# Pair attention on one core: the outputs of a past pair ahead of scores and transposed scores in each half slot

## The chip, the cores and the metric

The kernel runs on one NeuronCore of a Trainium2 chip. Its engines work side by side, each in the order of its own instruction stream, and wait for each other on semaphores: PE is TensorE (matmuls; PEld is its weight loads), DVE is VectorE, ACT is ScalarE, POOL is GpSimd, SP issues DMAs. The metric is the device time of one execution in microseconds (us); lower is better.

## The reference

The program is four layers of cross attention and feed-forward over `x` (8 batches, 256 tokens, width 128) with a context of 8 x 512 tokens. Two of the eight phases have the shape that the change touches, 16 heads of width 8, with 256 queries and 512 keys in each of the 8 batches. Cut to these:

```python
def _L1_xattn_ref(values, keys, query, mask, Wv, Wk, Wq, Wo, bo):
    v = (values @ Wv.T).reshape(n, -1, H, D)
    k = (keys @ Wk.T).reshape(n, -1, H, D)
    q = (query @ Wq.T).reshape(n, lq, H, D)
    score = jnp.einsum('nqhd,nkhd->nhqk', q, k)
    score = jnp.where(mask == 0, jnp.float32(-1e+20), score)
    attn = jax.nn.softmax(score / jnp.sqrt(jnp.float32(D)), axis=-1)
    out = jnp.einsum('nhqk,nkhd->nqhd', attn, v).reshape(n, lq, H * D)
    return out @ Wo.T + bo

def _L3_xattn_ref(query, key, value, temporal_bias, wq, bq, wk, bk, wv, bv, wo, bo):
    logits = jnp.einsum('bhqd,bhkd->bhqk', q, k) / scale
    logits = logits + temporal_bias[:, None, None, :]
    attn = jax.nn.softmax(logits, axis=-1)
    ...
x = x + _L1_xattn_ref(ctx_1024, ctx_1024, _layernorm(x, axis=-1), mask, ...)
...
x = x + _L3_xattn_ref(_layernorm(x, axis=-1), ctx_1024, ctx_1024, fside_BxS2_0, ...)
```

## The kernel before

Nine phases run one after the other. `pair_attention` (line 758) builds two of them: tag `l1x`, with a mask (`masked`), and tag `l3x`, with a bias of the keys in place of a mask (`biased`). I call them the masked and the biased attention.

Its unit is a pair of heads. There are 8 pairs in a batch and 8 batches, so T = 64 pairs, numbered t. All engines walk the same slots t = -7 .. 69, each cut into two half slots j = 0, 1. I number half slots h = 2t + j. A pair passes through these steps:

- `scores(t + LEAD, j, (w,))`, seven slots early: one matmul for each head w of the pair, from 128 queries against 512 keys, into bank `s_ps[w]`. Their only use is the row maximum, which DVE takes (`maximum`, lines 1069 and 1072) and which frees the bank.
- After four pairs, POOL splits their maxima into three bf16 parts (`mparts`, lines 643 to 649), PE turns them (job MX, line 1220), ACT copies them, and two DMAs put them as extra rows under the queries.
- `transposed_scores(t, j, (1 - w,))`: the scores again, with keys on the partitions and the maximum already taken off, into `st_ps[j]` (line 1255). In the masked attention `mask_scores(t, j)` first puts the mask into that bank (line 1242) and the transposed scores are added to it.
- ACT: `exponential(t, j)` reads `st_ps[j]` and writes `pT` (line 1131). It does so one half slot later in its own order.
- `outputs(group, c)`: a group is two pairs, that is four heads. For each of four chunks c of 128 keys, four heads' outputs and softmax sums are accumulated into the single bank `pv_ps` (line 1282). Chunks 0 to 3 of group g stand in half slots 4g + 4 to 4g + 7, so each half slot has one chunk.
- ACT: `copy_outputs(g)` (line 1139) takes the finished group out of `pv_ps`.
- `fill(job, b, n)`: small jobs through the one bank `misc`, at most one in a half slot: XT and Q make the queries of a batch, K and V its keys and values, MX turns maxima, OT, ONT and OUT finish a batch.

Two waits and one place in ACT's order matter. Chunk 0 of a group overwrites `pv_ps`, so it waits for the copy of the group before:

```python
pe.wait_ge(*m.exp_done.after(2 * (2 * group + 1) + c // 2 + 1))
if c == 0:
    if group:
        pe.wait_ge(*m.pv_copied.after(group))
```

And ACT's loop has that copy behind the exponential of the half slot before:

```python
before = t - 1 + j
if 0 <= before < T:
    exponential(before, 1 - j)
if j == 0 and t >= 4 and t % 2 == 0 and (t - 4) // 2 < T // 2:
    copy_outputs((t - 4) // 2)
job, b, half = filled_at.get(2 * t + j - 1, (None, 0, 0))
```

So at h = 8, 12, 16, .., 128 (31 of them) ACT does `exponential` of half slot h - 1, then the copy of the group that ended at h - 1, then the drain of the job of h - 1. The jobs of a batch b stand at 16b - 35 (K), 16b - 34 (XT), 16b - 32 (Q), 16b - 1 (V), 16b - 5 and 16b + 2 (MX), 16b + 20 and 16b + 22 (OT), 16b + 24 (ONT), 16b + 25 (OUT).

Of the kernel before, what the change touches and what calls it, by code (L numbers as in the profile page):

```python
# [757 lines left out]
def pair_attention(m, tag, wq, wk, wv, wo, bo, bq=None, bk=None, bv=None, mask=None, mask_t=None, key_bias=None, follow=None):  # L758
# [3 lines left out]
    T = B * PP  # L762
# [29 lines left out]
    with ExitStack() as ctx:  # L792
# [62 lines left out]
        with nc.Block() as block:  # L855
            @block.sync
            def _(sp):
# [13 lines left out]
                def stack_k(b, w):  # L871
                    if w == 0:
                        sp.wait_ge(*m.k_split.after(b - 1))
                        if b >= NST:
                            sp.wait_ge(*m.st_filled.after(2 * PP * (b - NST + 1)))
                    for row, _, of_k in STACK:
                        sp.dma_start(kT[b % NST][64 * w + row:64 * w + row + HD, :, :], parts[64 * w:64 * w + 64, of_k, 0:KV])\
                            .then_inc(m.stack_landed[b % NST].sem, 16)
                    if biased:
                        sp.dma_start(kT[b % NST][64 * w + 48:64 * w + 51, :, :],  # L880
                                     kb_rows[3 * b:3 * b + 3, :].unsqueeze(1).to_broadcast([3, PP, KV]))\
                            .then_inc(m.stack_landed[b % NST].sem, 16)
# [74 lines left out]
            def _(pool):  # L957
# [79 lines left out]
                for _, step, args in sorted(order, key=lambda s: s[0]):  # L1037
                    step(*args)
# [156 lines left out]
            def _(pe):  # L1195
# [39 lines left out]
                def mask_scores(t, j):  # L1235
                    b, p = divmod(t, PP)
                    if t >= 1:
                        pe.wait_ge(*m.exp_done.after(2 * t + j - 1))
                    if p == 0 and j == 0:
                        pe.wait_ge(*m.mask_t_ready.after(b + 1))  # L1240
                    for w in range(2):
                        pe.matmul(st_ps[j][:, w, :], k["ident_bf"], maskT_b[b % 2][:, 2 * j:2 * j + 2, :].rearrange("p c t -> p (c t)"),  # L1242
                                  start=True, stop=False)

                def transposed_scores(t, j, heads=(0, 1)):
                    b, p = divmod(t, PP)
                    if t >= 1 and heads[0] == FIRST_TURNED and not masked:
                        pe.wait_ge(*m.exp_done.after(2 * t + j - 1))
                    if j == 0 and p % 4 == 0 and heads[0] == FIRST_TURNED:
                        pe.wait_ge(*landed(m.max_moved, 2 * b + p // 4, 32))  # L1250
                    for e in range(2):
                        c = 2 * j + e
                        for w in heads:
                            rows = slice(64 * w, 64 * w + R2)
                            ins = pe.matmul(st_ps[j][:, w, e * S:(e + 1) * S], kT[b % NST][rows, p, c * P:(c + 1) * P], q[b % NST][rows, p, :],  # L1255
                                            start=not masked, stop=not masked or e == 1)
                    if len(heads) == 2 or heads[0] != FIRST_TURNED:
                        ins.then_inc(m.st_filled.sem, 1)

                def scores(t, j, heads=(0, 1)):  # L1260
                    b, p = divmod(t, PP)
                    if p == 0 and j == 0 and heads[0] == 0:
                        pe.wait_ge(*stack_landed(b))
                        if b < 2:
                            pe.wait_ge(*first.landed[b])
                    for w in heads:
                        if 2 * t + j >= 1:
                            pe.wait_ge(*m.s_drained[w].after(2 * t + j))
                        rows = slice(64 * w, 64 * w + R1)
                        pe.matmul(s_ps[w][:], q[b % NST][rows, p, j * P:(j + 1) * P], kT[b % NST][rows, p, :], start=True, stop=True)\  # L1270
                            .then_inc(m.s_filled[w].sem, 1)

                def outputs(group, c):
                    b, g = divmod(group, 4)
# [4 lines that stand above are left out]
                        if g == 0:  # L1279
                            pe.wait_ge(*is_drained(V, b, 0))  # L1280
                    for hh in range(4):
                        ins = pe.matmul(pv_ps[32 * hh:32 * hh + 32, 0:S], v[b % NV][:, c, (4 * g + hh) * 32:(4 * g + hh + 1) * 32],  # L1282
                                        pT[(2 * group + hh // 2) % 4][:, hh % 2, c, :], start=(c == 0), stop=(c == CPB - 1))
                    if c == CPB - 1:
                        ins.then_inc(m.pv_done.sem, 1)
# [11 lines left out]
                for t in range(-LEAD, LAST_SLOT + 1):  # L1297
                    for j in range(2):
                        if masked and 0 <= t < T:
                            mask_scores(t, j)  # L1300
                        for w in range(2):
                            if t + LEAD < T:
                                scores(t + LEAD, j, (w,))
                            if 0 <= t < T:
                                transposed_scores(t, j, (1 - w,))
                        if t >= 2 and (t - 2) // 2 < T // 2:
                            outputs((t - 2) // 2, 2 * (t % 2) + j)
                        if 2 * t + j in filled_at:
                            fill(*filled_at[2 * t + j])

# [2219 lines left out]
```

## Time and profile before

| | |
|---|---|
| time, median of 3 runs | 1832.46 us (1831.83 to 1833.85) |
| the profiled execution: its own time | 1837.7 us |
| its span in the trace | 1835.5 us |
| TensorE busy in the span | 1614.3 us, 88% |
| VectorE, ScalarE, GpSimd busy | 1298.6, 1051.9, 550.8 us |
| masked attention, pairs in flight | about 168 to 414 us of the span |
| biased attention, pairs in flight | about 1568 to 1781 us of the span |

The trace names an instruction by its line, the tile that it writes and the tiles that it reads. In the biased attention `pT` and the copied outputs lie in tiles that belong to other phases, so `pT` reads as `kT_l2x_first` or `v_l2x_first` and the copy (line 1139) as `wk_l2x_first` or `wv_l2x_first`. A timeline row gives the start, the duration, the engine, the line, and in brackets for how long the engine was idle before it and what ended that. "issue" means that the profile shows nothing that it waited for. Weight loads (PEld) start where PE turns to the next matmul, so their starts are the clearest marks of PE's progress.

### The profile page before, as it was taken

Reading aid. Unit: us, or ns where it says so; the run is one execution under the profiler, and the core shown is the slowest. Engines: PE = TensorE matmul, PEld = TensorE weight load, DVE = VectorE, ACT = ScalarE, POOL = GpSimd, SP = SyncE. Lnnn points to the kernel's source line nnn. Section 1 sums busy time; section 2 is a strip of 40 time slices with the busy share of each in tenths; the row PEclk is TensorE's granted clock in tenths of the full one; section 3 lists DMA queues with packets and bytes.
Section 4 is the critical chain, followed back from the end, with each engine's and each line's share of the span. In section 5 each row is a group of like instructions: output and inputs, shape, how many; then the busy total and the mean of one; then the engine's idle time right before and its main releaser. Section 6 shows DMA issues by size and latency. Waiting matters only on the chain. (4 is left out here: it accounts for less than half of the span.)

```text
span 1835.5 us, 32822 instructions
## 1 busy us (share of the span) xinstructions
PE 1614.3 (88%) x11034; PEld 884.1 (48%) x11084; DVE 1298.6 (71%) x3515; ACT 1051.9 (57%) x2283; POOL 550.8 (30%) x634
## 2 busy tenths in 40 slices
PE   5867999996799999999999879987789986999976
PEld 4532444433455555555555456664566653333333
DVE  5637788858766666666666868866788756789847
ACT  2322666667555555655555458873488740677764
POOL 0317565411100000000000168834588512433200
PEclk9896999997799999999999989998999996799997
DMA  5124333201100000000000000001100001322100
GB/s 160 41 38 131 80 69 75 46 2 46 36 1 7 7 1 7 6 1 26 1 1 1 1 7 0 0 1 45 44 4 0 1 14 27 82 47 51 34 2 23
DMA packets 60239, 53.46 MB, mean 29 GB/s; under 512 B 9610, under 2 KB 52798, under 8 KB 59974
## 3 DMA queue, kind: packets, MB, share of 16 engines
q1 hardware_dynamic: 59238, 51.30, 11.8%
q8 instruction: 79, 1.29, 0.3%
q14 instruction: 58, 0.48, 0.1%
q10 hardware_dynamic: 864, 0.39, 0.1%
HBM read 30.57 MB, written 1.05 MB: 17 GB/s over the span
## 5 line engine op out<-in xcount | busy, mean ns | idle before, releaser
L1771 DVE CUSTOM_DVE_ANT_0 minus_s_l2x<-s_ps_l2x,mask_b_l2x 128x512 f32<-128x512 f32 x256 | 166.5, 688 | 176.9 <-PE s_ps_l2x L1987 176.7
L1896 ACT ACTIVATE probs_l2x<-minus_s_l2x,nmax_l2x 128x512 f32<-128x512 f32 x256 | 182.7, 714 | 178.3 <-DVE nmax_l2x L1771 178.3
L1069 DVE CUSTOM_DVE_ANT_0 junk_l1x<-s_ps_l1x,mask_b_l1x 128x512 f32<-128x512 f32 x256 | 166.3, 687 | 49.8 <-PE s_ps_l1x L1270 45.6
L1072 DVE TENSOR_REDUCE nmax_l3x<-s_ps_l3x 128x1 f32<-128x512 f32 x256 | 163.8, 684 | 33.5 <-PE s_ps_l3x L1270 31.5
L1131 ACT ACTIVATE pT_l1x<-st_ps_l1x 128x1024 f32<-128x1024 f32 x128 | 131.0, 1023 | 79.3 <-PE st_ps_l1x L1255 78.9
L1844 DVE COPY pT_l2x<-t_ps_l2x 128x512 f32<-128x512 f32 x256 | 164.3, 683 | 0.5 <-PE t_ps_l2x L1996 0.5
L1996 PEld LDWEIGHTS t_ps_l2x<-consts,probs_l2x 128*128 128x128 f32 x1024 | 109.6, 141 | 98.6 <-issue 78.0
L1996 PE MATMUL t_ps_l2x<-consts,probs_l2x 128*128 128x128 f32 x1024 | 139.8, 280 | 1.9 <-ACT probs_l2x L1896 1.9
L2582 POOL TENSOR_TENSOR rn_l2a_first<-ssc_l2a_first,consts 128x16 f32<-128x16 f32 x28 | 108.5, 3876 | 34.2 <-DVE ssc_l2a_first L2609 33.7
L2752 ACT ACTIVATE probs_l2a<-minus_s_l2a,nmax_l2a 128x128 f32<-128x128 f32 (+1 forms) x256 | 105.8, 417 | 10.3 <-DVE nmax_l2a L2657 9.0
L2657 DVE CUSTOM_DVE_ANT_0 minus_s_l2a<-s_ps_l2a,consts 128x128 f32<-128x128 f32 (+1 forms) x256 | 66.8, 316 | 52.3 <-PE s_ps_l2a L2867 47.8
L2538 POOL TENSOR_TENSOR v_l2x_first<-kT_l2x_first,tb_l2a_first 128x256 f32<-128x256 f32 x112 | 96.7, 890 | 14.8 <-ACT kT_l2x_first L2720 14.3
L1270 PE MATMUL s_ps_l3x<-kT_l3x_first,q_l3x 51*128 51x512 bf16 x192 | 75.3, 435 | 15.1 <-DVE nmax_l3x L1072 8.2
L1282 PE MATMUL pv_ps_l1x<-pT_l1x,v_l1x 128*32 128x256 f32 x1024 | 81.2, 391 | 1.0 <-ACT o_l1x L1139 0.9
L1131 ACT ACTIVATE v_l2x_first<-st_ps_l3x 128x1024 f32<-128x1024 f32 x64 | 65.2, 1023 | 24.3 <-PE st_ps_l3x L1255 24.3
L1131 ACT ACTIVATE kT_l2x_first<-st_ps_l3x 128x1024 f32<-128x1024 f32 x64 | 65.3, 1023 | 20.9 <-PE st_ps_l3x L1255 20.2
L1987 PE MATMUL s_ps_l2x<-kT_l2x,q_l2x 64*128 64x512 f32 x256 | 72.3, 641 | 5.0 <-DVE nmax_l2x L1771 5.0
L1270 PE MATMUL s_ps_l1x<-kT_l1x_first,q_l1x 48*128 48x512 bf16 x192 | 65.9, 415 | 11.9 <-DMA q_l1x<-parts_l1x_first 8.4
L1987 PE MATMUL s_ps_l2x<-kT_l2x_first,q_l2x 64*128 64x512 f32 x256 | 73.2, 649 | 3.0 <-ACT q_l2x L1874 1.5
L1723 POOL TENSOR_TENSOR out_rs_l2x<-out_ve_l2x,consts 128x2 f32<-128x2 f32 x8 | 5.7, 707 | 223.6 <-DVE out_ve_l2x L1803 223.6
L1242 PE MATMUL st_ps_l1x<-maskT_b_l1x,consts_bf 128*128 128x512 bf16 x215 | 68.1, 383 | 4.7 <-issue 3.2
L1255 PE MATMUL st_ps_l3x<-q_l3x,kT_l3x_first 54*128 54x256 bf16 x384 | 65.8, 285 | 0.0
(539 smaller groups left out, 3784.2 us busy)
## 6 DMA issues: line engine op xcount, KB each, us to landing
mask_i_l1x<-in_mask SPq DMA_DIRECT2D x8, 512.0 KB, 3.9
maskT_i_l1x<-in_mask_t SPq DMA_DIRECT2D x8, 512.0 KB, 4.6
kT_l1x_first<-parts_l1x_first SPq DMA_DIRECT2D x60, 64.0 KB
kT_l3x_first<-parts_l3x_first SPq DMA_DIRECT2D x60, 64.0 KB
q_l1x<-parts_l1x_first SPq DMA_DIRECT2D x90, 32.0 KB
q_l3x<-parts_l3x_first SPq DMA_DIRECT2D x90, 32.0 KB
ctxT_l0x<-in_ctxT SPq DMA_DIRECT2D x9, 256.0 KB, 3.0
rows_l0x<-in_ctx SPq DMA_DIRECT2D x9, 256.0 KB, 4.0
```

What stands on the lines that cost most here:

```text
L1069: dve.tensor_tensor_reduce(out=junk[w][:], in0=s_ps[w][:], in1=mask_b[b % 2][:, j, :], scale=-1.0, scalar=3e38, op0=ALU.add, op1=ALU.min, ...
L1072: dve.tensor_reduce(to, s_ps[w][:], AX.X, ALU.max, negate=True).then_inc(m.s_drained[w].sem, 1)
L1131: act.activation(pT[t % 4][:, :, 2 * j:2 * j + 2, :].rearrange("p w c t -> p w (c t)"), st_ps[j][:], ACT.Exp)\
L1270: pe.matmul(s_ps[w][:], q[b % NST][rows, p, j * P:(j + 1) * P], kT[b % NST][rows, p, :], start=True, stop=True)\
L1771: dve.tensor_tensor_reduce(out=minus_s[n % 4][:], in0=s_ps[n % 2][:], in1=mask_b[b % 2][:], scale=-1.0, scalar=3e38, op0=ALU.add, op1=ALU. ...
L1844: dve.tensor_copy(pT[g % 2][:, hh, :, j * P:(j + 1) * P], t_ps[c % 2][:].rearrange("p (c t) -> p c t", t=P))\
L1896: act.activation(probs[n % 4][:], minus_s[n % 4][:], ACT.Exp, bias=nmax[:, b % 2, n:n + 1], scale=-1.0, accum_out=sums[:, b % 2, j, h:h + ...
L1987: pe.matmul(s_ps[n % 2][:], q[b % 2][rows, g, j * P:(j + 1) * P], kT[b % 2][rows, g, :], start=True, stop=True)\
L1996: ins = pe.transpose(t_ps[n % 2][:, c * P:(c + 1) * P], probs[n % 4][:, c * P:(c + 1) * P], k["ident"])
L2538: eng.tensor_tensor(other[:, j, w, :, to], qk[:, j, w, :, of], tb[:, w, j, to].unsqueeze(1).to_broadcast([P, NH, 32]), ALU.mult).then_inc( ...
L2582: pool.tensor_tensor(rn[:, cols], ssc[:, cols], k["minus_half"][:, 0:2 * NH], ALU.pow).then_inc(m.powers_ready.sem, 1)
L2752: act.activation(probs[n % (2 * DEEP)][:, cols], minus_s[n % (2 * DEEP)][:, cols], ACT.Exp, bias=nmax[:, u, TPB * n + j:TPB * n + j + 1], ...
```

## The change

In both attentions the call of `outputs` moves from behind the scores and transposed scores of its half slot to ahead of them. In the masked attention it then stands between the mask's matmuls and the scores. Which group and chunk a half slot works on is unchanged, and so are all waits inside the steps. The jobs of `fill` stay last in the half slot.

```diff
                     for j in range(2):
                         if masked and 0 <= t < T:
                             mask_scores(t, j)
+                        if t >= 2 and (t - 2) // 2 < T // 2:
+                            outputs((t - 2) // 2, 2 * (t % 2) + j)
                         for w in range(2):
                             if t + LEAD < T:
                                 scores(t + LEAD, j, (w,))
                             if 0 <= t < T:
                                 transposed_scores(t, j, (1 - w,))
-                        if t >= 2 and (t - 2) // 2 < T // 2:
-                            outputs((t - 2) // 2, 2 * (t % 2) + j)
                         if 2 * t + j in filled_at:
                             fill(*filled_at[2 * t + j])
```

On PE, masked attention, half slots 11 (an MX job at its end) and 12 (chunk 0 of group 2), before:

```order
L1282 MATMUL pv_ps_l1x<-pT2_l1x,v0_l1x 32x256 x2
L1282 MATMUL pv_ps_l1x<-pT3_l1x,v0_l1x 32x256 x2
L1220 MATMUL misc_l1x<-consts_bf,mparts_l1x 24x128 x2
L1242 MATMUL st_ps0_l1x<-maskT_b0_l1x,consts_bf 128x512 x2
L1270 MATMUL s_ps0_l1x<-kT1_l1x_first,q1_l1x 128x512
L1255 MATMUL st_ps0_l1x<-q0_l1x,kT0_l1x_first 128x256 x2
L1270 MATMUL s_ps1_l1x<-kT1_l1x_first,q1_l1x 128x512
L1255 MATMUL st_ps0_l1x<-q0_l1x,kT0_l1x_first 128x256 x2
L1282 MATMUL pv_ps_l1x<-pT0_l1x,v0_l1x 32x256 x2
L1282 MATMUL pv_ps_l1x<-pT1_l1x,v0_l1x 32x256 x2
```

The same two half slots on PE after the change, again from the outputs of half slot 11 to those of half slot 12:

```order
L1282 MATMUL pv_ps_l1x<-pT2_l1x,v0_l1x 32x256 x2
L1282 MATMUL pv_ps_l1x<-pT3_l1x,v0_l1x 32x256 x2
L1270 MATMUL s_ps0_l1x<-kT1_l1x_first,q1_l1x 128x512
L1255 MATMUL st_ps1_l1x<-q0_l1x,kT0_l1x_first 128x256 x2
L1270 MATMUL s_ps1_l1x<-kT1_l1x_first,q1_l1x 128x512
L1255 MATMUL st_ps1_l1x<-q0_l1x,kT0_l1x_first 128x256 x2
L1220 MATMUL misc_l1x<-consts_bf,mparts_l1x 24x128 x2
L1242 MATMUL st_ps0_l1x<-maskT_b0_l1x,consts_bf 128x512 x2
L1282 MATMUL pv_ps_l1x<-pT0_l1x,v0_l1x 32x256 x2
L1282 MATMUL pv_ps_l1x<-pT1_l1x,v0_l1x 32x256 x2
```

Between the last transposed scores of half slot 11 (into `st_ps1`) and chunk 0 of the next group there stood the outputs of half slot 11, the MX job, the mask, two scores and four transposed scores. Now there stand the MX job and the mask alone.

On PE in the biased attention, the same half slots 11 and 12 before:

```order
L1282 MATMUL pv_ps_l3x<-v_l2x_first,v0_l3x 32x256 x4
L1220 MATMUL misc_l3x<-consts_bf,mparts_l3x 24x128 x2
L1270 MATMUL s_ps0_l3x<-kT1_l3x_first,q1_l3x 128x512
L1255 MATMUL st_ps0_l3x<-q0_l3x,kT0_l3x_first 128x256 x2
L1270 MATMUL s_ps1_l3x<-kT1_l3x_first,q1_l3x 128x512
L1255 MATMUL st_ps0_l3x<-q0_l3x,kT0_l3x_first 128x256 x2
L1282 MATMUL pv_ps_l3x<-kT_l2x_first,v0_l3x 32x256 x4
```

And after:

```order
L1282 MATMUL pv_ps_l3x<-v_l2x_first,v0_l3x 32x256 x4
L1270 MATMUL s_ps0_l3x<-kT1_l3x_first,q1_l3x 128x512
L1255 MATMUL st_ps1_l3x<-q0_l3x,kT0_l3x_first 128x256 x2
L1270 MATMUL s_ps1_l3x<-kT1_l3x_first,q1_l3x 128x512
L1255 MATMUL st_ps1_l3x<-q0_l3x,kT0_l3x_first 128x256 x2
L1220 MATMUL misc_l3x<-consts_bf,mparts_l3x 24x128 x2
L1282 MATMUL pv_ps_l3x<-kT_l2x_first,v0_l3x 32x256 x4
```

Here, without a mask, chunk 0 follows the transposed scores of the half slot before directly, or with that half slot's job between.

On ACT, masked attention, the rows that go with half slots 11 to 13. They are the same before and after:

```order
L1131 ACTIVATE pT1_l1x<-st_ps0_l1x 128x2x512 [waits pv_done,st_filled]
L1131 ACTIVATE pT1_l1x<-st_ps1_l1x 128x2x512 [waits st_filled]
L1139 ACTIVATE o0_l1x<-pv_ps_l1x 128x256 [waits pv_done]
L1172 ACTIVATE mT0_l1x<-misc_l1x 24x256 [waits max_moved_even,misc_filled]
L1131 ACTIVATE pT2_l1x<-st_ps0_l1x 128x2x512 [waits pv_done,st_filled]
```

The copy of the group's outputs (line 1139) stands behind the exponential of half slot 11, which reads `st_ps1`. Nothing moved here.

## Rows read from the trace of the kernel before

**Rows 1.** The page: span, and busy time of each engine.

```profile
span 1835.5 us, 32822 instructions
PE 1614.3 (88%) x11034; PEld 884.1 (48%) x11084; DVE 1298.6 (71%) x3515; ACT 1051.9 (57%) x2283; POOL 550.8 (30%) x634
```

**Rows 2.** Windows: stretch, its length, busy of PE, PEld, DVE, ACT, POOL; then the clock.

```profile
168.00:410.00 242.00, 232.97 (x2151) 95.58 (x2190) 185.91 (x635) 156.15 (x203) 116.55 (x139) 1.00 0.29 61
1568.00:1777.00 209.00, 192.22 (x1938) 76.72 (x1936) 171.35 (x352) 156.21 (x204) 64.86 (x120) 0.97 0.22 43
```

**Rows 3.** Waits, 170 to 390 us: who waited for whom; us, times, longest.

```profile
PEld s_ps_l1x L1270 <- DVE nmax_l1x L1069: 6.9, 16, 0.5
```

**Rows 4.** Waits, 1570 to 1760 us.

```profile
PEld s_ps_l3x L1270 <- DVE nmax_l3x L1072: 49.2, 112, 0.8
```

**Rows 5.** Timeline, masked attention: half slots 7 and 8 of a batch.

```profile
275.19 0.16 PEld L1282 LDWEIGHTS pv_ps_l1x<-pT_l1x,v_l1x 128*32 128x32 f32 x8 [0.21 <-issue]
...
275.34 1.02 ACT L1131 ACTIVATE pT_l1x<-st_ps_l1x 128x1024 f32<-128x1024 f32 x1 [1.10 <-PE st_ps_l1x L1255]
...
275.76 0.11 PEld L1242 LDWEIGHTS st_ps_l1x<-maskT_b_l1x,consts_bf 128*128 128x128 bf16 x2 [0.41 <-issue]
...
276.26 0.38 ACT L1139 ACTIVATE o_l1x<-pv_ps_l1x 128x256 f32<-128x256 f32 x1
276.29 0.09 PEld L1270 LDWEIGHTS s_ps_l1x<-kT_l1x_first,q_l1x 48*128 48x128 bf16 x1 [0.42 <-issue]
...
276.84 0.16 PEld L1282 LDWEIGHTS pv_ps_l1x<-pT_l1x,v_l1x 128*32 128x32 f32 x8 [0.21 <-issue]
```

**Rows 6.** Timeline, masked attention: the last group's chunk 0.

```profile
410.41 0.16 PEld L1282 LDWEIGHTS pv_ps_l1x<-pT_l1x,v_l1x 128*32 128x32 f32 x8 [0.21 <-issue]
...
411.45 0.38 ACT L1139 ACTIVATE o_l1x<-pv_ps_l1x 128x256 f32<-128x256 f32 x1
411.94 0.15 PEld L1282 LDWEIGHTS pv_ps_l1x<-pT_l1x,v_l1x 128*32 128x32 f32 x5 [1.37 <-ACT pT_l1x L1131]
411.98 0.42 PE L1282 MATMUL pv_ps_l1x<-pT_l1x,v_l1x 128*32 128x256 f32 x4 [0.92 <-ACT o_l1x L1139]
```

**Rows 7.** Timeline, biased attention: half slots 7 and 8 of a batch.

```profile
1663.24 1.27 DVE L1072 TENSOR_REDUCE nmax_l3x<-s_ps_l3x 128x1 f32<-128x512 f32 x2
1663.32 0.16 PEld L1282 LDWEIGHTS pv_ps_l3x<-kT_l2x_first,v_l3x 128*32 128x32 f32 x8 [0.21 <-issue]
...
1664.89 0.18 PEld L1282 LDWEIGHTS pv_ps_l3x<-v_l2x_first,v_l3x 128*32 128x32 f32 x8 [0.21 <-issue]
```

**Rows 8.** Timeline, masked attention: half slot 15 with the V job, and 16.

```profile
290.52 0.16 PEld L1282 LDWEIGHTS pv_ps_l1x<-pT_l1x,v_l1x 128*32 128x32 f32 x8 [0.21 <-issue]
...
292.61 0.09 PEld L1270 LDWEIGHTS s_ps_l1x<-kT_l1x_first,q_l1x 48*128 48x128 bf16 x1 [0.42 <-issue]
...
293.15 0.16 PEld L1282 LDWEIGHTS pv_ps_l1x<-pT_l1x,v_l1x 128*32 128x32 f32 x8 [0.21 <-issue]
```

**Rows 9.** Timeline, biased attention: half slot 15 with the V job, and 16.

```profile
1649.21 0.16 PEld L1282 LDWEIGHTS pv_ps_l3x<-kT_l2x_first,v_l3x 128*32 128x32 f32 x8 [0.21 <-issue]
...
1650.87 0.09 PEld L1270 LDWEIGHTS s_ps_l3x<-kT_l3x_first,q_l3x 51*128 51x128 bf16 x1
...
1651.41 0.16 PEld L1282 LDWEIGHTS pv_ps_l3x<-v_l2x_first,v_l3x 128*32 128x32 f32 x8 [0.21 <-issue]
```

**Rows 10.** Timeline, masked attention: half slot 2 of a batch, its MX job, half slot 3.

```profile
296.97 0.16 PEld L1282 LDWEIGHTS pv_ps_l1x<-pT_l1x,v_l1x 128*32 128x32 f32 x8 [0.21 <-issue]
...
297.88 0.12 PEld L1220 LDWEIGHTS misc_l1x<-consts_bf,mparts_l1x 128*24 128x24 bf16 x2 [0.76 <-issue]
...
299.19 0.16 PEld L1282 LDWEIGHTS pv_ps_l1x<-pT_l1x,v_l1x 128*32 128x32 f32 x8 [0.21 <-issue]
```

**Rows 11.** Windows: two stretches of other phases with a less busy PE.

```profile
1300.00:1340.00 40.00, 27.30 (x152) 18.73 (x151) 31.14 (x63) 23.18 (x59) 27.59 (x32) 0.87 0.22 52
1440.00:1480.00 40.00, 35.03 (x293) 25.55 (x292) 26.17 (x95) 29.28 (x106) 11.60 (x16) 1.00 0.00 1
```

## The prediction, made before the changed kernel was run

> **What bounds the kernel now.** I read the page first: TensorE is the busiest engine, 88% of the span, and the next is VectorE with 71% [rows 1]. That is a mean over nine phases, so I then cut out the two stretches in which the change acts. In the masked attention PE is busy for 233.0 of 242 us, at the full clock; in the biased one for 192.2 of 209 us, with VectorE at 171.4 [rows 2]. The waits say the rest. In the masked attention PE waited for VectorE's release of a score bank for 6.9 us in all, so nothing but PE sets the pace there [rows 3]. In the biased one, without the mask's matmuls, it waited so for 49.2 us, 112 times: PE and VectorE pace each other through two score banks [rows 4]. ScalarE has room in both.
>
> Then the timeline, for one plain half slot. I take as its mark E the start of the output's weight loads, by which every transposed score of the half slot has been issued. In the masked attention from E(7) = 275.19: outputs take 0.57 (to 275.76), the mask 0.53 (to 276.29), scores and transposed scores 0.55 (to 276.84), sum 1.65 us [rows 5]. In the biased one E(7) to E(8) is 1663.32 to 1664.89, 1.57 us [rows 7].
>
> **The wait that the change runs into.** Nothing is added or removed; 128 blocks of outputs move in each attention. What counts is what each waits for. The exponentials that chunk 0 needs are those that the mask or the transposed scores of its half slot need anyway, so they cost nothing. The other wait is for the copy of the group before, and ACT comes to that copy only behind the exponential of half slot h - 1, which itself cannot start before the last transposed score of h - 1, that is before E. The chain is in [rows 5]: exponential at E + 0.15, copy 0.92 later, 0.38 long, so done at E + 1.45. How long PE takes from there is seen where it already waits, at the last group: the copy ends at 411.45 + 0.38 = 411.83, the loads start at 411.94, 0.11 later [rows 6]. Chunk 0 can start at E + 1.56 and not earlier.
>
> Before, it starts at E + 1.65 in the masked and E + 1.57 in the biased attention: the wait just fits, and costs nothing, because the outputs of h - 1 and all other matmuls of h lie ahead. After the change E comes behind those outputs, and between E and chunk 0 stand only the mask's 0.53 us, or nothing at all. So:
>
> - masked, plain: from E to the next E is 1.56 + 0.57 (outputs) + 0.55 (scores) = 2.68 instead of 1.65: **+1.03 us**.
> - biased, plain: 2.68 instead of 1.57: **+1.11 us**. VectorE does not hide it: its two reductions of half slot 7 run from 1663.24 to 1664.51 [rows 7], and the next score would be issued at 1663.32 + 1.56 + 0.57 = 1665.45. It stands idle with PE, and after the stall the two go on in the old rhythm, whose PE waits return.
> - behind a V job: masked, V and mask together last from 290.52 + 0.57 = 291.09 to 292.61, 1.52 us, which hides nearly all: 2.68 instead of 2.63, +0.05 [rows 8]. Biased: 2.68 instead of 1651.41 - 1649.21 = 2.20, +0.48 [rows 9].
> - the last group waited before, 1.53 us from E [rows 6]; now its predecessor's outputs no longer lie in that wait: 1.56 + 0.57 - 1.53 = +0.60.
>
> Queued behind the waiting chunk on PE are the scores for VectorE and the transposed scores for ScalarE; both engines run dry, so nothing makes the time good.
>
> There are 31 chunks 0 that wait (h = 8 to 128). 7 stand behind a V job, one is the last, 23 are plain. Masked: 23 x 1.03 + 7 x 0.05 + 0.60 = 24.6. Biased: 23 x 1.11 + 7 x 0.48 + 0.60 = 29.5.
>
> **The jobs that lose their cover.** `fill` now follows E directly, 0.57 us earlier against it. The MX job of half slot 2 already waits for POOL: its loads start at E + 0.91, where E + 0.57 was PE's turn, and E(3) follows 1.31 later [rows 10]. POOL's result depends on scores whose distance to E is unchanged, so it comes at E + 0.91 again, and the outputs, which filled 0.57 of that wait, are now to be done behind it: +0.57, seven times in each attention (in batch 0 no outputs run yet), 4.0 us each. I price the biased one alike. The other jobs wait for ScalarE or VectorE with more room; I put nothing on them, and up to 0.2 us each as the upper bound.
>
> **Sum.** 24.6 + 29.5 + 8.0 = 62.1 us. I take off 2: a third of the 6.9 us of VectorE waits in the masked attention may fall into a stall [rows 3], and the other MX job (0.27 us) stands inside the stall at half slot 12. That leaves +60. On the profiled execution's 1837.7 us this gives 1898; that execution is 5.2 us above the median 1832.5, so against the runs I forecast 1892.5.
>
> A row and a rule: while PE waited for the copy, its weight loads did not go ahead either. They had been idle for 1.37 us and began 0.04 before the first matmul [rows 6]. The Trainium skill, "TensorE: Matmul & The Clock Gate", section "The mechanism" in Part 3, says that weight loads are pulled ahead of matmuls in flight and that matmuls keep strict order. By that, the loads would be done within the stall, saving some 0.04 x 62 = 2.5 us, and the time would be 1890; the row decides against it, and its strict order of matmuls agrees with the scores having to wait behind the outputs.
>
> **Bounds.** Low: the bare exponential and copy without any handoff, 0.92 + 0.38 = 1.30 for 1.56, over 46 plain stalls takes off 12: 1880. High: four more jobs a batch each wait 0.2 us, 2 x 8 x 4 x 0.2 = 13: 1905. The main case's own range is 1880 to 1905.
>
> **Rivals.**
>
> 1. *VectorE covers the stall in the biased attention.* For it: PE spends 49.2 us there in waiting for VectorE [rows 4], which looks like slack. Against it: VectorE finishes 0.94 us before the next score in my reckoning above. If it held, only the masked share and one MX term, 24.6 + 4.0 = 29, would remain: 1861.
> 2. *The clock falls.* PE would be busy for about 192 of 242 us in the biased attention, 0.79. A stretch at 0.68 busy has a mean granted clock of 0.87, one at 0.88 has 1.00 [rows 11]. At 0.87 about a quarter of 242 us would run at 1.2 GHz, the lower of the two levels; there the 1.12 us of PE work in a half slot lasts up to twice as long, half of it hidden by waits: some 15 to 20 us more, 1910. Against it: the stalls are near 1 us, and between them PE is dense.
> 3. *The wait is met after all*, so that nothing changes but the MX terms: 1832 to 1840. It needs the copy to be done before E + 0.53; the chain gives E + 1.45.
> 4. *Faster.* In the masked attention the outputs now stand between the mask and the scores, which gives VectorE 0.57 us more for its banks after the mask. If the copy came in time, the 6.9 us of those waits would go: 1826. It decides at the same point: the copy done by E + 0.53 in the masked attention, and by E in the biased one.
>
> **How the numbers follow.** Main case 0.78 (1892), rival 1 0.08, rival 2 0.08, rival 3 0.03, rival 4 0.03. The range reaches down to rival 1, since a partly covered stall lies between it and the main case, and up to 1908, short of rival 2: 1860 to 1908. About 0.2% (some 4 us) is what a measurement of this kernel can tell from no change. Faster takes rival 4, 0.03; same takes most of rival 3, 0.03; slower has the rest, 0.94.
>
> **What the profile of the changed kernel would show.** Chunk 0 (line 1282) preceded by an idle PEld of about 1 us in the masked and 1.5 us in the biased attention, put down to ScalarE's copy (line 1139) or the exponential before it, about 30 times in each; E to E 2.68 at such half slots, unchanged at the three others; a stretch of the masked attention longer by some 28 us, of the biased one by some 32; the other seven phases as before; VectorE's idle time before scores up by about as much; the MX job of half slot 2 still at E + 0.9. The prediction is wrong if chunk 0 starts earlier than E + 1.4, if the half slots behind a stall run shorter than before and win it back, if the waits of jobs grow by more than the MX term, or if the granted clock of either stretch drops.

## The result and the profile after

The changed kernel takes 1915.03 us (median of 4 runs, 1912.44 to 1917.91) against 1832.14 us (4 runs, 1830.6 to 1833.85) for the kernel before on the same chip: the medians are 83 us apart. The ratio worked out from the runs is 1.0438, 95% interval 1.0425 to 1.045, which is some 80 us, a little less than the medians say; both are used below, and where kernels are compared it is the ratio. The forecast was +60 and a time of 1892; the end of its range, 1908, is 7 us too low. The profiled execution took 1916.62 us.

The page of the changed kernel, span and busy times, then the granted clock in tenths for 40 slices of the span (answers to [rows 1]):

```profile
span 1914.4 us, 32822 instructions
...
PE 1633.3 (85%) x11034; PEld 888.4 (46%) x11084; DVE 1306.1 (68%) x3515; ACT 1050.3 (55%) x2283; POOL 551.2 (29%) x634
...
PEclk9886999997799999999999999998999986898987
```

The number of instructions is the same, 11034 matmuls among them, and so are the busy times of VectorE, ScalarE and GpSimd within 8 us. PE's busy time went up by 19.0 us with no matmul added: on average they took longer.

The two attentions as windows (columns as in [rows 2]; the first is the masked attention, the second the biased one, the third the biased one without its ends):

```profile
171.00:441.00 270.00, 236.70 (x2159) 96.47 (x2198) 188.35 (x635) 154.29 (x203) 116.39 (x138) 1.00 0.24 54
1598.00:1857.00 259.00, 208.46 (x1948) 83.94 (x1946) 177.69 (x352) 156.28 (x204) 65.14 (x120) 0.89 0.18 35
1600.00:1840.00 240.00, 192.59 (x1798) 78.45 (x1794) 172.95 (x337) 143.57 (x189) 63.07 (x117) 0.89 0.18 34
```

Their ends are those of the transposed scores, as the view of line 1255's instructions gives them (count, shortest, median and longest in ns, first and last start in us):

```profile
L1255 PE MATMUL st_ps_l1x<-q_l1x,kT_l1x_first x384: 267/271/418, 171.4 to 441.4; 51*128 51x256 bf16 x192
L1255 PE MATMUL st_ps_l3x<-q_l3x,kT_l3x_first x384: 267/279/418, 1597.9 to 1856.9; 54*128 54x256 bf16 x192
```

Before, these two stretches were 168.7 to 410.2 and 1567.8 to 1777.1. So the masked attention went from 241.5 to 270.0 us, **+28.5**, and the biased one from 209.3 to 259.0, **+49.7**; the spans differ by 78.9, which leaves about 0.7 for all the rest (what lies ahead of the masked attention took 2.7 longer, other phases gave 2.0 of it back). The medians differ by 4 us more than the spans, since the profiled execution of before lay 5.6 us above its median and this one 1.6.

In the masked attention PE is busy for 3.7 us more in a stretch that is 28.5 longer: waits. In the biased one it is busy for 16 us more, and the granted clock is 0.89 where it was 0.97.

Cut finer, the clock says more. The first two rows are the biased attention before, the last two after (the clock is the third number from the end):

```profile
1570.00:1600.00 30.00, 27.50 (x246) 10.04 (x243) 22.41 (x37) 21.81 (x29) 10.48 (x19) 0.80 0.27 59
1600.00:1630.00 30.00, 27.52 (x283) 11.18 (x275) 25.94 (x52) 22.32 (x30) 12.78 (x24) 1.00 0.29 50
1600.00:1630.00 30.00, 24.81 (x217) 9.16 (x214) 20.17 (x33) 19.45 (x26) 9.72 (x17) 0.83 0.26 56
1690.00:1720.00 30.00, 24.86 (x243) 10.55 (x239) 24.17 (x51) 18.40 (x24) 10.34 (x18) 0.94 0.25 43
```

Before, only the start of this attention ran at a lowered clock; each later stretch of 30 us was at 1.00. After the change no such stretch of the attention is above 0.94.

**A stall in the masked attention** (timeline, the start of a group; start, duration, then in brackets the idle time before it and what ended it):

```profile
289.81 0.11 PEld L1242 LDWEIGHTS st_ps_l1x<-maskT_b_l1x,consts_bf 128*128 128x128 bf16 x2 [0.21 <-issue]
...
289.96 1.02 ACT L1131 ACTIVATE pT_l1x<-st_ps_l1x 128x1024 f32<-128x1024 f32 x1 [1.20 <-PE st_ps_l1x L1255]
...
290.88 0.38 ACT L1139 ACTIVATE o_l1x<-pv_ps_l1x 128x256 f32<-128x256 f32 x1
...
291.37 0.19 PEld L1282 LDWEIGHTS pv_ps_l1x<-pT_l1x,v_l1x 128*32 128x32 f32 x8 [1.45 <-ACT pT_l1x L1131]
...
291.97 0.09 PEld L1270 LDWEIGHTS s_ps_l1x<-kT_l1x_first,q_l1x 48*128 48x128 bf16 x1 [0.41 <-issue]
...
292.51 0.20 PEld L1229 LDWEIGHTS misc_l1x<-consts,on_l1x 128*128 128x128 f32 x2 [0.21 <-issue]
```

E is now where the mask's weight loads begin, 289.81. The exponential starts at E + 0.15, the copy at E + 1.07, chunk 0 at 291.37 = E + 1.56: the forecast to the hundredth. Everything that stands behind chunk 0 on PE waits with it; the next mark E, here the loads of a job at 292.51, comes 2.70 after this one (2.68 was forecast). It is not this stall alone: read in the same way, at each of the 60 copies that start within the two attentions' windows chunk 0 starts 1.51 to 1.57 us after E.

**A stall in the biased attention** (the same view):

```profile
1680.18 1.02 ACT L1131 ACTIVATE v_l2x_first<-st_ps_l3x 128x1024 f32<-128x1024 f32 x1 [0.68 <-PE st_ps_l3x L1255]
1681.10 0.38 ACT L1139 ACTIVATE wk_l2x_first<-pv_ps_l3x 128x256 f32<-128x256 f32 x1
...
1681.59 0.19 PEld L1282 LDWEIGHTS pv_ps_l3x<-v_l2x_first,v_l3x 128*32 128x32 f32 x8 [1.78 <-ACT v_l2x_first L1131]
1681.62 0.64 PE L1282 MATMUL pv_ps_l3x<-v_l2x_first,v_l3x 128*32 128x256 f32 x8 [1.52 <-ACT wk_l2x_first L1139]
...
1682.62 1.29 DVE L1072 TENSOR_REDUCE nmax_l3x<-s_ps_l3x 128x1 f32<-128x512 f32 x2 [0.92 <-PE s_ps_l3x L1270]
```

Here no mask fills the beginning. The weight loads' idle time, 1.78, holds the 0.21 that stands before them anyway; the rest, 1.57, is the whole way from E to chunk 0. VectorE sat idle for 0.92 us before the scores that came behind it (0.94 was forecast): it did not cover the stall. The loads started 0.03 us before the first matmul, not during the wait, as in [rows 6]. In each attention 23 chunks 0 wait so (weight loads idle for 1.22 to 1.78 us), and at all 46 the loads start 0.03 or 0.04 us before the matmul.

**Another one, 24 us later,** in which the clock is down:

```profile
1703.96 1.02 ACT L1131 ACTIVATE kT_l2x_first<-st_ps_l3x 128x1024 f32<-128x1024 f32 x1 [0.64 <-PE st_ps_l3x L1255]
...
1704.88 0.38 ACT L1139 ACTIVATE wk_l2x_first<-pv_ps_l3x 128x256 f32<-128x256 f32 x1
...
1705.36 1.08 PE L1282 MATMUL pv_ps_l3x<-kT_l2x_first,v_l3x 128*32 128x256 f32 x8 [1.48 <-ACT kT_l2x_first L1131]
...
1706.37 0.60 PE L1270 MATMUL s_ps_l3x<-kT_l3x_first,q_l3x 51*128 51x512 bf16 x1
1706.38 0.81 PE L1255 MATMUL st_ps_l3x<-q_l3x,kT_l3x_first 54*128 54x256 bf16 x3
```

The wait is the same, but then eight output matmuls take 1.08 us instead of 0.64, three transposed scores 0.81 instead of 0.49: PE runs at the lower of its two levels, 1.2 GHz for 2.4; the granted clock from 1705.30 to 1707.50 is 0.51, and it was 1.00 from 1703.00 to 1705.30. From chunk 0's start to the end of the half slot it takes about 2.0 us where it took 1.1.

**The waits of the MX job,** from the view of line 1220 over the whole span:

```profile
POOL mparts_l3x L649: 7.9, 8
POOL mparts_l1x L649: 7.6, 8
```

Before:

```profile
POOL mparts_l3x L649: 3.8, 8
POOL mparts_l1x L649: 3.6, 8
```

The rise, 4.1 and 4.0, is the forecast's 4.0 each.

### The profile page after: what moved, and what is told of

It reads as the page before. It is cut to its first block and busy times, and to the rows that moved or that the text cites. A ratio compares the mean times of both kernels' runs of the same rounds, so it can differ in the third digit from the quotient of the medians.

```text
span 1914.4 us, 32822 instructions
## 1 busy us (share of the span) xinstructions
PE 1633.3 (85%) x11034; PEld 888.4 (46%) x11084; DVE 1306.1 (68%) x3515; ACT 1050.3 (55%) x2283; POOL 551.2 (29%) x634
## 5 line engine op out<-in xcount | busy, mean ns | idle before, releaser
L1282 PE MATMUL pv_ps_l3x<-kT_l2x_first,v_l3x 128*32 128x256 f32 x512 | 51.2, 478 | 20.9 <-ACT kT_l2x_first L1131 10.3
```

## The experiments

Theory A: the loss is the wait of chunk 0 for ScalarE's copy (and, behind it, the lost cover of the MX job); in the biased attention the lowered clock comes on top. Rivals: the parts act on each other (one attention's change disturbs the other); the loss comes from having the outputs ahead at all and not from the copy; the clock fell for some other reason than the pauses. The kernels of these experiments are numbered 1 to 6 by their headings. All ratios are to the kernel before on the same chip, whose median was 1835.52 us beside the first four kernels and 1834.35 beside the last four.

**1. Only the masked attention, only the biased one.** The condition of the early outputs:

```
-                        if t >= 2 and (t - 2) // 2 < T // 2:
+                        if masked and t >= 2 and (t - 2) // 2 < T // 2:
```

with the call at its old place for the other attention; `biased` for `masked` in the second kernel.

> The change in the masked attention alone. Theory (every chunk 0 waits 1.56 us behind E for ScalarE's copy, and each attention pays for itself): the masked stretch grew by 28.5 us in the changed kernel's trace, so the time is about 1861 us (+29), with the biased attention's length and clock as before. Rival (the loss is one of the clock, which the first attention starts and the second goes on with): the biased attention is slower here too, and the time is above 1870 us.

> The change in the biased attention alone. Theory: the biased stretch grew by 49.7 us in the changed kernel's trace, 33.5 us of it by the waits that the prediction priced and some 16 us by a granted clock of 0.89 where it was 0.97, so the time is about 1881 us (+50), with the clock of that stretch near 0.89. Rival (that clock was a matter of one execution, or was handed on by the masked attention): the clock stays near 0.97 and the time is about 1866 us (+34).

Masked only: 1866.55 us, ratio 1.016 [1.0139, 1.0181], +31; the masked attention takes 270.0 us as in the changed kernel, the biased one 208.3. Biased only: 1884.90 us, ratio 1.0272 [1.0253, 1.0292], +49; masked 242.2, biased 257.7. The two add up: 31 + 49 = 80 us, as the ratios have it for both together (0.016 + 0.0272 beside 0.0438). The windows, masked and then biased attention in the first kernel,

```profile
172.00:442.00 270.00, 236.70 (x2161) 96.49 (x2202) 188.31 (x635) 154.25 (x202) 115.84 (x138) 1.00 0.25 53
1600.00:1800.00 200.00, 183.19 (x1854) 73.19 (x1853) 168.25 (x342) 149.06 (x195) 63.06 (x118) 0.98 0.22 42
```

and the biased attention in the second:

```profile
1575.00:1820.00 245.00, 195.88 (x1867) 79.68 (x1867) 172.41 (x344) 146.98 (x193) 60.14 (x111) 0.90 0.16 31
```

The clock falls in the biased attention with the change there alone (0.90), and does not when only the masked one is changed (0.98). So the low clock belongs to the biased attention's own stalls.

**2. Chunk 0 at its old place, chunks 1 to 3 ahead.**

```
-                        if t >= 2 and (t - 2) // 2 < T // 2:
+                        if 2 * (t % 2) + j > 0 and t >= 2 and (t - 2) // 2 < T // 2:
```

The call with the opposite condition stands at the old place, behind the scores.

> As the changed kernel, but chunk 0 of a group stays behind the scores, where it was before; chunks 1 to 3 stay ahead of them. Theory (the wait for the copy is the cost, and it hangs on chunk 0 alone): the stalls are gone and only the MX job of half slot 2 loses its cover, seven times 0.57 us in each attention, so +8: about 1840 us, and the clock of the biased attention is back at 0.97. Rival (outputs ahead of scores cost something by themselves, since VectorE and ScalarE get their matmuls 0.57 us later in each half slot): three of four half slots still pay, and the time stays above 1860 us.

1869.04 us, ratio 1.018 [1.0163, 1.0197], +33.5: a miss for the theory and the rival alike. The copy's stall is gone and the biased attention's clock is up at 0.94 (0.97 before), yet the masked attention takes 257.7 us (+16.2 over before), the biased one 227.5 (+18.2). A cause lies in the experiment's own edit: chunk 0 stays behind its scores while chunk 1, of the next half slot, comes ahead of its own, so the two stand together, and one half slot of each four has no outputs. The weight loads of the biased attention show the pair (x16 instead of x8):

```profile
1694.00 0.62 PEld L1282 LDWEIGHTS pv_ps_l3x<-kT_l2x_first,v_l3x 128*32 128x32 f32 x16 [0.24 <-issue]
```

and the waits of the masked attention, 180 to 400 us, show what the empty half slot costs (6.9 us, 16 times, in [rows 3]):

```profile
PEld s_ps_l1x L1270 <- DVE nmax_l1x L1069: 22.1, 48, 0.5
```

PE comes to the scores of the empty half slot too early for VectorE's bank and waits, up to 0.5 us, and gets nothing back from the double half slot; that the loss comes about in this way is argued from these rows, not shown. An estimate of 0.57 us for each of 31 groups is 17.7 us. But the 16.2 and 18.2 that were measured hold the waits of the MX job as well, here

```profile
POOL mparts_l3x L649: 8.3, 8
POOL mparts_l1x L649: 7.3, 8
```

for 3.8 and 3.6 before. Without their growth 12.5 and 13.7 us are left, 0.40 and 0.44 for each group.

**3. Two chunks at the old place.** The same edit with `> 1` for `> 0`, so that chunks 0 and 1 stay behind. If the loss in 2 comes from one bunching for each group, it stays; if it comes from the number of chunks that stand ahead, it falls by a third.

> As the kernel with chunk 0 left behind the scores (+33 us, where +8 was expected), but with chunks 0 and 1 behind and only 2 and 3 ahead. Theory formed from that run (in each group one half slot has no outputs in front of its scores, so PE has nothing to do while VectorE frees its banks, and the next has two chunks together, while VectorE and ScalarE run dry; once a group, whichever chunks they are): about the same +33 us, 1.018. Rival (each chunk ahead of the scores costs something by itself, three of four before and two of four now): two thirds of it, +22 us, 1.012.

1864.71 us, ratio 1.0167 [1.0148, 1.0186], +30.5. The intervals of 2 and 3 overlap, and a fall by a third (to +22, a ratio of 1.012) lies outside of this one. The traces are less clear. The attentions take 254.3 and 221.5 us, which is +12.8 and +12.2 where kernel 2 had +16.2 and +18.2: together 25.0 for 34.4. A part of the fall is the MX job, which waits less here:

```profile
POOL mparts_l3x L649: 6.6, 8
POOL mparts_l1x L649: 3.8, 8
```

Without the growth of these waits the masked attention loses 12.6 us, as in kernel 2 (12.5), both at a clock of 1.00: there it is one bunching for each group, whichever chunks stand ahead. The biased one loses 9.4 for 13.7, and its clock (0.95 for 0.94) differs little: there the question stays open.

**4. The copy ahead of the exponential.** The changed kernel, and on ScalarE:

```
-                        if 0 <= before < T:
-                            exponential(before, 1 - j)
                         if j == 0 and t >= 4 and t % 2 == 0 and (t - 4) // 2 < T // 2:
                             copy_outputs((t - 4) // 2)
+                        if 0 <= before < T:
+                            exponential(before, 1 - j)
```

The last outputs of a group are now issued ahead of the transposed scores, so the copy has its data before the exponential has; in this order it no longer stands behind 0.92 us of exponential.

> As the changed kernel, but ScalarE does the copy of a finished group ahead of the exponential of the half slot before, not behind it. Theory: the outputs of that half slot are now early, so the copy can be done about 0.1 us behind E; chunk 0 no longer waits in the masked attention and some 0.2 us in the biased one, and with the MX term the time is about 1843 us (+8 to +14). Rival (the exponential, now 0.3 us later, is what PE waits for next, or chunk 0 waited for something else than this copy): the time stays above 1870 us.

1844.64 us, ratio 1.0051 [1.0035, 1.0068], +9: of the 80 us of the ratio 71 are gone (of the medians' 83, 74) with this one order on ScalarE, the outputs being as early as in the changed kernel. The masked attention takes 248.0 us (+6.5), the biased one 211.6 (+2.3) at a clock of 0.99. What ends the idle time of the engines before the instructions on the outputs' tile, biased attention (the weight loads' and the matmuls' idle time are counted apart; `issue` is no wait that the profile shows), first in the changed kernel, then here:

```profile
ACT kT_l2x_first L1131: 34.3, 22
issue: 22.7, 78
ACT v_l2x_first L1131: 19.1, 18
ACT wk_l2x_first L1139: 13.0, 12
ACT wv_l2x_first L1139: 12.7, 11
```

```profile
issue: 23.1, 88
PE pv_ps_l3x L1282: 1.7, 6
ACT kT_l2x_first L1131: 1.5, 4
ACT v_l2x_first L1131: 1.1, 5
```

This separates "outputs ahead of scores" from "chunk 0 behind the copy": the second costs nearly all, and of the 9 us that the first leaves, about 8 is the growth of the MX waits (7.8 and 7.6 us here, for 3.8 and 3.6).

**5. The pauses filled.** The changed kernel, and ahead of chunk 0's wait for the copy in the biased attention six matmuls into the next transposed-score bank, which real ones overwrite:

```
                     if c == 0:
                         if group:
+                            if biased:
+                                stay_awake(m, pe, st_ps[0][:, 0, :], 6)
                             pe.wait_ge(*m.pv_copied.after(group))
```

> The changed kernel, and in the biased attention PE does six matmuls of 512 columns into a free bank ahead of each wait of chunk 0 for the copy. At the full clock they fill some 1.3 of the 1.57 us of the stall, so they delay nothing; their results are written over. Theory (16 us of the change's loss is the granted clock of 0.89 in that stretch, which falls because PE pauses): the clock is back near 0.97 and the time is about 1899 us against 1915 of the changed kernel, that is a ratio to the kernel before near 1.036. Rival (the waits alone account for the 50 us of the biased attention, and the clock is a bystander): the time stays at 1915 us, ratio 1.044, or rises if the added matmuls reach past the stall.

1902.88 us, ratio 1.0378 [1.0359, 1.0397], against 1.0438 without them: 11 us less by the ratios, 12 by the medians; in the traces the biased attention takes 244.3 us for 259.0, 14.7 less. The window of the biased attention,

```profile
1600.00:1840.00 240.00, 223.29 (x2090) 90.04 (x2090) 175.09 (x350) 151.75 (x200) 63.70 (x118) 0.99 0.19 34
```

and one stall, with E at 1706.01:

```profile
1706.01 0.98 PEld L451 LDWEIGHTS st_ps_l3x<-consts_bf 128*128 128x128 bf16 x6 [0.21 <-issue]
...
1706.16 1.02 ACT L1131 ACTIVATE v_l2x_first<-st_ps_l3x 128x1024 f32<-128x1024 f32 x1 [0.84 <-PE st_ps_l3x L1255]
1707.08 0.38 ACT L1139 ACTIVATE wv_l2x_first<-pv_ps_l3x 128x256 f32<-128x256 f32 x1
...
1707.51 0.16 PEld L1284 LDWEIGHTS pv_ps_l3x<-v_l2x_first,v_l3x 128*32 128x32 f32 x8 [0.52 <-ACT wv_l2x_first L1139]
```

Chunk 0 starts at E + 1.50 here; PE does useless work instead of pausing, and the clock stays up.

What is left of the biased attention's loss, 244.3 - 209.3 = 35.0 us, isn't the waits and the MX term alone, for two reasons. Behind a V job there was hardly a pause to fill, and the six matmuls stand in the way:

```profile
1689.44 1.02 ACT L1131 ACTIVATE v_l2x_first<-st_ps_l3x 128x1024 f32<-128x1024 f32 x1 [0.25 <-PE st_ps_l3x L1255]
...
1690.18 1.07 PEld L451 LDWEIGHTS st_ps_l3x<-consts_bf 128*128 128x128 bf16 x6
1690.30 1.46 PE L451 MATMUL st_ps_l3x<-consts_bf 128*128 128x512 bf16 x6
...
1691.68 0.16 PEld L1284 LDWEIGHTS pv_ps_l3x<-v_l2x_first,v_l3x 128*32 128x32 f32 x8 [0.42 <-issue]
```

Chunk 0 starts at E + 2.39, at all seven such places within 0.01 us, where the changed kernel had E + 1.56: 7 x 0.83 = 5.8 us are the experiment's own. And its clock is better than that of the kernel before (0.99 for 0.97), which by an estimate is worth at most 4 us: some 8 us less at half speed. So the waits and the MX term come to 35.0 - 5.8 = 29, up to 33, where 29.5 + 4.0 = 33.5 was forecast, and of the 49.7 us some 16 to 20 are the clock's. This split is an estimate; that filling the pauses brings the clock back and 11 us with it is measured.

**6. The MX job a half slot later,** on kernel 4 and, alone, on the kernel before:

```
-        jobs += [(16 * b - 1, V, b, 0), (16 * b - 5, MX, b, 0), (16 * b + 2, MX, b, 1), (16 * b + 20, OT, b, 0),
+        jobs += [(16 * b - 1, V, b, 0), (16 * b - 5, MX, b, 0), (16 * b + 3, MX, b, 1), (16 * b + 20, OT, b, 0),
```

> ScalarE's copy ahead of the exponential, and the MX job of half slot 2 moved to half slot 3 (16b + 3), so that POOL's result is there when PE comes to it. Theory (what is left of the loss with the copy first is the MX job's lost cover, seven times 0.57 us in each attention): 5 to 8 us faster than with the copy first alone, at 0.5 per cent above the kernel before, so a ratio of 1.001 or less. Rival (the rest is something else, such as the exponential that now comes later): no gain, ratio 1.005.

> The kernel before, with only the MX job of half slot 2 moved to half slot 3. Before, PE waits for POOL there by about 0.34 us, seven times in each attention. Theory: up to 5 us faster, ratio 0.997 to 1.000. Rival (the maxima reach the queries too late when turned one half slot later): slower, with waits of the transposed scores for the DMAs.

On kernel 4: 1831.79 us (12 runs), ratio 0.9984 [0.997, 0.9997]. That is 0.0067 less than kernel 4, some 12 us, more than the 5 to 8 expected. On the kernel before: 1828.31 us (11 runs), ratio 0.997 [0.9957, 0.9982], 5.5 us less than the kernel before, with the outputs where they were. The second explains the first, if the two effects add: 5.5 of the 12 us are the wait for GpSimd that the kernel before had already, and the 7 that remain are the cover that the change took from the job, forecast as 8.0. In the first of the two GpSimd ended the idle time before line 1220 only once:

```profile
POOL mparts_l3x L649: 0.3, 1
```

Early outputs with both repairs (0.9984) are no better than late outputs with the one (0.997); the intervals overlap, so that they are worse is not shown either.

Giving `pv_ps` a second buffer, so that chunk 0 needs no copy, wasn't tried.

## Why the prediction was right in direction and too low

- **The wait that the change runs into:** right. Chunk 0 starts 1.51 to 1.57 us after E at all 60 places (1.56 forecast), with the copy as the last step of the chain. Kernel 4, which takes the exponential out of that chain, gives back 71 of 80 us.
- **masked, plain, behind a V job, the last group:** 24.6 + 4.0 = 28.6 us forecast for the masked attention, 28.5 measured, at a clock of 1.00. That it fits to 0.1 us is partly chance: kernel 4 gives back 22.0 us of it and the MX waits grew by 4.0, so 2.5 us of what was priced as waits for the copy have another cause or are the price of kernel 4's own order.
- **biased, plain and behind a V job:** 29.5 + 4.0 = 33.5 forecast, 29 to 33 by kernel 5, where the clock is kept up. In the whole attention, however, 49.7 were lost.
- **The jobs that lose their cover:** 8.0 forecast; 8.1 by the waits for GpSimd, 7 by experiment 6.
- **Sum:** the 2 us taken off for waits that fall into a stall did not show in the masked attention, which lost 28.5 us for 28.6 without them.
- **Rival 1,** that VectorE covers the stall: wrong, for the reason given there; VectorE was idle for 0.92 us at its end.
- **Rival 2,** that the clock falls: this happened, *along with* the main case. Its numbers were near: a clock of 0.87 forecast and 0.89 measured, PE busy 0.79 of the stretch and 0.80 measured, 15 to 20 us more; filling the pauses gave back 11 to 15, and the estimate for the clock's whole share is 16 to 20.

**The step that failed** is in "Rivals" and "How the numbers follow": the fall of the clock was entered as an alternative of 0.08, with the range drawn "short of rival 2", on the ground that "the stalls are near 1 us, and between them PE is dense". That sentence is true of the masked attention, whose clock did stay at 1.00. In the biased one the same text had derived a stall of 1.56 us with no mask to shorten it, and had worked out a busy share of 0.79, beside a row at 0.68 with a clock of 0.87 [rows 11]. By its own numbers the case stood between the two rows of that group, and deserved something near even odds; and rival 2 was no alternative to the main case but a term to be added to it. What the runs showed in its place: the clock of the biased attention fell to 0.89 and took some 16 to 20 of the 49.7 us. The account of the +83: 60 forecast; 2 wrongly taken off; 16 more in the biased attention (49.7 for 33.5), the clock's 16 to 20 less the up to 4 by which the waits were priced too high; 1 for the rest of the span. That makes 79, the difference of the spans; the last 4 are the profiled executions' places among the runs.

## What to carry to other kernels

Before moving work ahead on one engine, walk the chain that frees its output buffer through the other engine's queue in that engine's order: here the copy stood behind an exponential that could not start before the very matmuls that were passed, and moving the copy with the outputs took the loss from some 80 to 9 us. When a change puts repeated pauses into TensorE, price them twice, as the pauses and, where rows of the kernel put the clock in doubt, as the matmuls behind them at the lower clock, and add the two. And when a chunk of a regular rhythm is moved and its neighbour isn't, an empty slot appears (kernels 2 and 3): in the masked attention its cost came once for each group, whether one chunk or two stayed behind.

## What the runs showed of the hardware

- The clock told the two attentions apart. Masked: PE busy 236.7 of 270 us (0.88), with pauses of about 1.0 us at the start of most groups: 1.00. Biased: busy 192.6 of 240 us (0.80), with pauses of up to 1.5 us: 0.89; no wait of PE there is longer. With six matmuls ahead of each chunk 0, busy 223.3 of 240 (0.93): 0.99. Whether the length of the pauses or the share decides, these runs don't tell, since both differ.
- Work of no use can save time: the six matmuls of kernel 5, ahead of each chunk 0, keep PE busy for 1.47 us, and the kernel is 11 us faster than without them.
- Weight loads did not go ahead while their matmuls waited for the copy: they began 0.03 or 0.04 us before the first of them in all 46 stalls, as 0.04 in [rows 6]. The Trainium skill, "TensorE: Matmul & The Clock Gate", section "The mechanism" in Part 3, has them pulled ahead of matmuls in flight; no matmul is in flight in these stalls, and no load starts early in them. Where matmuls are in flight, the trace agrees with the page: in kernel 5, in the stall behind a V job, the loads of the six matmuls start at 1690.18, 0.12 us before their first matmul and while the job's matmuls still run (to 1690.46).
